# Four MLPs with their matmuls in three single passes over rounded parts and rests

## The chip, the cores and the metric

One NeuronCore of a Trainium2 chip runs the whole kernel. The metric is the device time of one execution in microseconds (us), taken as the median of several runs. TensorE multiplies, VectorE, ScalarE and GpSimd work elementwise, and SyncE issues the DMAs. In the profile they are PE (PEld for its weight loads), DVE, ACT, POOL and SP.

## The reference

Four layers on a residual x of 4 x 256 tokens of width 256 (8 tiles of 128 tokens). Each is an attention followed by an MLP:

- L0: attention over 320 keys, then an MLP behind an RMS norm.
- L1 and L3: two cross attentions each over 64 context keys (four in all, called a = 0 to 3), then an MLP behind a layer norm.
- L2: one cross attention with heads of 16, then an MLP behind a layer norm.

What the change touches is the MLP:

```python
h = _layer_norm(x, ln_mlp_scale, ln_mlp_offset)
h = jax.nn.gelu(h @ w_fc1 + b_fc1, approximate=False) @ w_fc2 + b_fc2
return x + h
```

w_fc1 is 256 x 1024 and w_fc2 1024 x 256, all in float32. L0 and L2 take the tanh form of gelu.

## The kernel before

It is written by hand, engine by engine, and every dependence is a semaphore. Each engine works through one fixed list in order, so an instruction that waits holds up all that stand behind it on its engine. The stages run one after the other: attention 0, mlp(0), keys(0) and tokens(0), keys(1) and tokens(1), mlp(1), attend2, mlp(2), keys(2) and tokens(2), keys(3) and tokens(3), mlp(3). The keys stages fold the weights of 16 heads, streamed by DMA; the tokens stages run over 8 token tiles.

**An MLP** works on four pairs b of token tiles (256 tokens each):

- VectorE: `mlp_spread` (L1367) takes the statistics of both tiles of a pair (L1355 in layer 0, L1357 to L1359 otherwise), `mlp_z` (L1373) writes the normalised z (L1364, L1365) once GpSimd's `power` (L449) has given 1/sqrt. It also adds the down product to x (L1428).
- TensorE: `turn(b)` (L925) transposes z, four 128x128 blocks. `up(b)` (L937) multiplies: for each of 8 blocks f of the hidden width and each half d of the input width, w1's 128x128 block is the stationary operand and hT (128x256) the moving one. In the middle of `up(b)` stands `turn(b + 1)`. `down(b)` (L950) multiplies for each of the two tiles u the 8 blocks of gelu's output hid (stationary) by w2's 128x256 (moving). The order is up(0), up(1), down(0), up(2), down(1), up(3), down(2), in even layers the first two heads' keys of the next stage (L697, L699), down(3).
- ScalarE: `turned(b)` (L1123) writes hT from the transposes, with scale and offset; gelu (L1134) writes hid, one 128x256 block at a time.
- GpSimd: `power`, and `add_row` (L409), which adds the second bias to x, two tiles a pair.

One float32 product of 128x128 by 128x256 stands in the trace as two MATMUL instructions, each with its own weight load. An fp32r product (a float32 rounded to fewer bits) stands as one. The kernel already has such products: the folded keys (L727) are made of a rounded part and the rest, in three passes `PASSES = ((0, 0), (0, 1), (1, 0))`, and attention 0 spreads its queries and keys with fp32r copies (L577, split on VectorE by L1286 and L1288 in `split0`).

**Attention 0** runs 64 steps. In each, GpSimd multiplies the probabilities by the inverse sums (L440), and TensorE turns and uses them (L602, L615). **A tokens stage** has for each tile: scores (L774), softmax on VectorE (L1490 to L1504), half of the multiplication by the inverse sums on GpSimd (L468), transposes (L786), output (L798), and the next tile's h from ScalarE (L1104). **attend2** has z (L1365), queries, softmax and outputs for each tile, and little on GpSimd.

w1 and w2 of a layer are loaded by SyncE (`load_mlp`, L345) as soon as the MLP before has ended, long before they are used. SBUF holds a large tile `arena`, which the stages share.

## Time and profile before

| | us |
|---|---|
| three timed runs | 1070.59, 1075.76, 1069.27 |
| their median | 1070.59 |
| the profiled execution, its own time | 1061.86 |
| its span, first to last instruction | 1060.1 |
| mean granted TensorE clock | 0.986 |

The profile is of one execution. Its time is 0.8% below the median of the timed runs, and 1.76 us of it lie outside the span. Times in the rows below are in us from the span's start; a mean duration of one instruction is in ns. Matmuls overlap, so that the mean duration of one is longer than the step from one to the next.

### The profile page before, as it was taken

Reading aid. Unit: us, or ns where it says so; the run is one execution under the profiler, and the core shown is the slowest. Engines: PE = TensorE matmul, PEld = TensorE weight load, DVE = VectorE, ACT = ScalarE, POOL = GpSimd, SP = SyncE. Lnnn points to the kernel's source line nnn. Section 1 sums busy time; section 2 is a strip of 40 time slices with the busy share of each in tenths; the row PEclk is TensorE's granted clock in tenths of the full one; section 3 lists DMA queues with packets and bytes.
Section 4 is the critical chain, followed back from the end, with each engine's and each line's share of the span. In section 5 each row is a group of like instructions: output and inputs, shape, how many; then the busy total and the mean of one; then the engine's idle time right before and its main releaser. Section 6 shows DMA issues by size and latency. Waiting matters only on the chain.

```text
span 1060.1 us, 15203 instructions
## 1 busy us (share of the span) xinstructions
PE 964.6 (91%) x5272; PEld 775.6 (73%) x5272; DVE 676.3 (64%) x1540; ACT 449.2 (42%) x1108; POOL 341.9 (32%) x381
## 2 busy tenths in 40 slices
PE   5789989799998999989899898899998989989898
PEld 4677778688785677857688687788875678756787
DVE  3788988511989849898511554313989859888510
ACT  3566667432554335633331343422653335533331
POOL 2644535410443324533321020111443324433210
PEclk8899999999999999999999998999999999999999
DMA  9000000000452004310000200200460004200000
GB/s 349 22 1 2 2 1 2 1 1 1 122 181 106 1 1 139 120 60 1 1 1 1 80 1 1 70 1 21 139 219 30 1 20 148 92 1 1 1 11 30
DMA packets 14382, 52.43 MB, mean 49 GB/s; under 512 B 1507, under 2 KB 3043, under 8 KB 13028
## 3 DMA queue, kind: packets, MB, share of 16 engines
q1 hardware_dynamic: 14308, 51.46, 14.3%
q8 instruction: 44, 0.72, 0.3%
q14 instruction: 30, 0.25, 0.1%
HBM read 50.41 MB, written 1.05 MB: 49 GB/s over the span
## 4 chain that ended last, share of the span: by engine, by line
PE 73%; DVE 11%; DMA 8%; issue 4%; ACT 3%; POOL 1%; SPq 0%; DVEq 0%; ACTq 0%
PE ps L950 10%; PE ps L774 9%; PE ps L798 9%; PE ps L937 9%; DMA ring<-in_heads_dram 8%; PE ps L697 4%; PE ps L615 4%; PE ps L699 3%; PE ps L738 3%; PE ps L602 3%; PE ps L727 3%; PE ps L786 2%; PE ps L591 2%; DVE pT_all L1313 2%; PE ps L844 2%
## 5 line engine op out<-in xcount | busy, mean ns | idle before, releaser
L774 PE MATMUL ps<-arena,hT 128*128 128x512 f32 x256 | 117.6, 603 | 15.3 <-ACT hT L1104 15.3
L1428 DVE TENSOR_TENSOR x<-ps,x 128x512 f32<-128x512 f32 x16 | 11.1, 692 | 182.7 <-PE ps L950 182.7
L798 PE MATMUL ps<-arena,pT_all 128*128 128x256 f32 x512 | 116.5, 381 | 7.5 <-ACT pT_all L1181 4.7
L937 PE MATMUL ps<-hT,w 128*128 128x256 f32 x512 | 114.8, 380 | 4.8 <-ACT hT L1123 4.8
L449 POOL TENSOR_TENSOR rstd<-var,neg_half 128x1 f32<-128x1 f32 (+1 forms) x56 | 36.4, 651 | 243.2 <-DVE var L1359 243.2
L950 PE MATMUL ps<-w,arena 128*128 128x256 f32 x512 | 113.3, 379 | 1.8 <-DVE x L1428 1.8
L440 POOL TENSOR_TENSOR arena<-arena,rinv 128x640 f32<-128x640 f32 x64 | 80.2, 1253 | 100.5 <-DVE rinv L1322 100.5
L798 PEld LDWEIGHTS ps<-arena,pT_all 128*128 128x128 f32 x512 | 94.7, 190 | 21.6 <-ACT pT_all L1181 5.7
L937 PEld LDWEIGHTS ps<-hT,w 128*128 128x128 f32 x512 | 96.0, 190 | 18.0 <-issue 5.6
L950 PEld LDWEIGHTS ps<-w,arena 128*128 128x128 f32 x512 | 97.1, 190 | 15.6 <-issue 2.5
L1134 ACT ACTIVATE arena<-ps,cols 128x256 f32<-128x256 f32 x128 | 53.7, 471 | 107.4 <-PE ps L937 107.4
L774 PEld LDWEIGHTS ps<-arena,hT 128*128 128x128 f32 x256 | 48.5, 192 | 65.4 <-issue 46.9
L468 POOL TENSOR_TENSOR prob<-prob,rinv 128x512 f32<-128x512 f32 x32 | 49.5, 1547 | 141.2 <-DVE rinv L1502 141.2
L1188 ACT ACTIVATE prob<-prob 128x512 f32<-128x512 f32 x32 | 20.2, 631 | 143.9 <-DVE prob L1492 143.9
L433 POOL TENSOR_TENSOR vacc<-vacc,vpart 128x256 f32<-128x256 f32 x60 | 44.1, 734 | 108.1 <-ACT vpart L1156 105.8
L1051 ACT ACTIVATE arena<-ps,nb 128x320 f32<-128x320 f32 x128 | 66.4, 523 | 27.0 <-DVE nb L1307 24.7
L697 PE MATMUL ps<-ctxT,ring 128*128 128x256 f32 x256 | 69.3, 393 | 7.5 <-DMA ring<-in_heads_dram 6.9
L1150 ACT ACTIVATE HL<-ps,kvd 128x256 fp32r<-128x256 f32 x64 | 30.5, 476 | 96.3 <-PE ps L699 96.3
L1307 DVE TENSOR_REDUCE nb<-ps 128x2 f32<-128x640 f32 x64 | 52.4, 820 | 25.4 <-PE ps L591 25.3
L602 PE MATMUL ps<-ident,arena 128*128 128x128 f32 x320 | 47.9, 281 | 21.1 <-DVE pT_all L1313 21.0
L727 PE MATMUL ps<-HL,wq 128*128 128x256 f32 x384 | 66.6, 309 | 0.4
L738 PE MATMUL ps<-ring,VT 128*128 128x256 f32 x256 | 65.9, 379 | 0.3 <-DVE x L1428 0.2
(151 smaller groups left out, 1955.0 us busy)
## 6 DMA issues: line engine op xcount, KB each, us to landing
ring<-in_heads_dram SPq DMA_DIRECT2D x64, 512.0 KB, 3.5
w<-in_w_dram SPq DMA_DIRECT2D x8, 1024.0 KB, 7.3
x<-in_x_dram SPq DMA_DIRECT2D x1, 1024.0 KB, 10.0
lnb<-in_lnb_dram SPq DMA_DIRECT2D x4, 256.0 KB, 9.2
ring<-in_wp_dram SPq DMA_DIRECT2D x1, 1024.0 KB, 4.9
out_dram<-x SPq DMA_DIRECT2D x4, 256.0 KB, 2.3
arena<-in_kinT_dram SPq DMA_DIRECT2D x1, 960.0 KB, 7.3
brow<-in_brow_dram SPq DMA_DIRECT2D x1, 768.0 KB, 11.0
```

Of the source, the lines that this page charges most:

```text
L440: g.tensor_tensor(w, w, rinv[:, n % 2, 0:2].unsqueeze(2).broadcast_to([P, 2, KEYS0]), ALU.mult)\
L602: last = nc.tensor.transpose(ps[:, 4 + c // 4, (c % 4) * P:(c % 4 + 1) * P], prob0[:, n % 4, c * P:(c + 1) * P], ident[:, :])
L697: mm(ps[:, k, 0:B * C], w[:, d * P:(d + 1) * P], ctxT[:, 0, d, :], start=(d == 0), stop=(d == 1))
L727: last = mm(ps[:, A_BANKS[k][d], 0:B * C], wq[:, k, c, d * P:(d + 1) * P], KT[:, k, e, :], start=(p == 0), stop=(p == 2))
L738: last = mm(ps[:, 5 + k, g * D:(g + 1) * D], VT[:, k, g * P:(g + 1) * P], ring[:, n % RING, 768:1024], start=True, stop=True)
L774: last = mm(ps[:, half, :], hT[:, k, d, 0:P], A[:, d, b // 2, cols_of, sl, :].rearrange("p r s k -> p r (s k)"), start=(d == 0), stop=(d = ...
L798: last = mm(ps[:, 6, 0:D], pT[:, k, c, :], VW[:, b, c, :], start=(c == 0), stop=(c == PAIRS - 1))
L937: last = mm(ps[:, f // 2, (f % 2) * 256:(f % 2 + 1) * 256], w1[:, d, f * P:(f + 1) * P], hT[:, k, d, :], start=(d == 0), stop=(d == 1))
L950: last = mm(ps[:, 5 + u, 0:D], hid[:, k, f, u * P:(u + 1) * P], w2[:, f, :], start=(f == 0), stop=(f == FT - 1))
L1051: last = a_(prob0[:, n % 4, e * KEYS0:(e + 1) * KEYS0], ps[:, 2 * (n % 2) + e, 0:KEYS0], ACT.Exp, bias=nb[:, n % 2, e:e + 1], scale=-1.0, ...
L1134: a_(hid[:, b % 2, f, :], ps[:, f // 2, (f % 2) * 256:(f % 2 + 1) * 256], gelu, bias=col(bias, f)).then_inc(hid_ready, 1)
L1307: v.tensor_reduce(nb[:, n % 2, :], ps[:, j:j + 2, 0:KEYS0], AX.X, ALU.min).then_inc(nb_ready, 1)
```

## The change

Every float32 product of the four MLPs is replaced by three fp32r products: high x high, high x low, low x high. The high part is the value rounded to fp32r, the low part the float32 difference, written as fp32r.

- **Weights.** GpSimd splits w1 and w2 into w1H, w1L, w2H, w2L with `split_weights(l, j)`, 16 instructions a layer on 128x512 each (even j a copy, odd j a subtraction). Layer 0's stand in attention 0 behind the multiplications of even steps 24 to 54; those of layers 1 and 3 in tokens(1) and tokens(3), two behind each tile's multiplication; those of layer 2 in attend2, four behind each of the tiles 4 to 7.
- **Activations.** VectorE splits hT (128x512) in `mlp_split(l, b)`, a copy and a subtraction; TensorE's `up(b)` waits for `hs_ready` where it waited for `hm_ready`. `mlp_split(l, 0)` stands ahead of the statistics of pair 1, and `mlp_split(l, b + 1)` behind the high copies of pair b's first half.
- **gelu's output.** VectorE writes hidH in four copies of 128x512 a pair (`hidden_high`), GpSimd the rest hidL in four subtractions of 128x512, in place of hid. `down(b)` waits for hidL, pair of blocks by pair of blocks.
- **Order.** VectorE's addition of pair b's result moves behind the high copies of pair b + 1. GpSimd's `power` of pair b + 2 moves to the head of pair b, and its memset (3.66 us, layer 1) from pair 0 to pair 1.
- **Places.** Several tiles share addresses (`overlay`), and x0 and prob0 move within `arena`.

The diff, without the semaphores' declarations:

```diff
+        def overlay(name, shape, dt):
+            with nc.sbuf_tensor(name, shape, dt) as tile:
+                return tile
+        arena_r = overlay("arena_r", [P, 16384], F32R)
-        x0 = arena[:, 11776:13824].rearrange("p (t n) -> p t n", t=TILES)
-        prob0 = arena[:, 13824:13824 + 4 * 2 * KEYS0].rearrange("p (k n) -> p k n", k=4)
+        prob0 = arena[:, 11776:11776 + 4 * 2 * KEYS0].rearrange("p (k n) -> p k n", k=4)
+        x0 = arena[:, 14336:16384].rearrange("p (t n) -> p t n", t=TILES)
-        copies = sb("copies", [P, 4, 2, 2, P], F32R)
-        K0 = sb("K0", [P, 3, KEYS0], F32R)
-        Q0 = sb("Q0", [P, 3, 2, S], F32R)
+        first_r = overlay("first_r", [P, 2048 + 3 * KEYS0 + 6 * S], F32R)
+        copies = first_r[:, 0:2048].rearrange("p (j w c n) -> p j w c n", j=4, w=2, c=2)
+        K0 = first_r[:, 2048:2048 + 3 * KEYS0].rearrange("p (k n) -> p k n", k=3)
+        Q0 = first_r[:, 2048 + 3 * KEYS0:2048 + 3 * KEYS0 + 6 * S].rearrange("p (k e n) -> p k e n", k=3, e=2)
+        PN = H * C + H
+        prob = sb("prob", [P, 2, PN])
+        wq = sb("wq", [P, 2, 2, D], F32R)
+        VT = sb("VT", [P, 2, B * C])
+        u = sb("u", [P, 2, D])
+        vpart = sb("vpart", [P, 2, D])
...
+        w1L = overlay("w1L", [P, DH, F], F32R)
+        w2L = overlay("w2L", [P, FT, D], F32R)
+        w1H = sb("w1H", [P, DH, F], F32R)
+        w2H = sb("w2H", [P, FT, D], F32R)
-        VT = sb("VT", [P, 2, B * C])
-        wq = sb("wq", [P, 2, 2, D], F32R)
+        hL = overlay("hL", [P, 2, DH, 2 * P], F32R)
+        hH = sb("hH", [P, 2, DH, 2 * P], F32R)
-        PN = H * C + H
-        prob = sb("prob", [P, 2, PN])
+        hidL = arena_r[:, 0:4096].rearrange("p (k f n) -> p k f n", k=2, f=FT)
+        hidH = arena_r[:, 9728:13824].rearrange("p (k f n) -> p k f n", k=2, f=FT)
...
-                sp.dma_start(w1[:, :, :], t["w1"][l]).then_inc(in_mlp, 16)
-                sp.dma_start(w2[:, :, :], t["w2"][l]).then_inc(in_mlp, 16)
+                sp.dma_start(w1[:, :, :], t["w1"][l]).then_inc(in_w1, 16)
+                sp.dma_start(w2[:, :, :], t["w2"][l]).then_inc(in_w2, 16)
...
                         pool.wait_ge(vacc_ready, n)
                         g.tensor_tensor(vacc[:, :], vacc[:, :], vpart[:, k, :], ALU.add).then_inc(vacc_ready, 1)
 
+            def split_weights(l, j):
+
+                c, high = j // 2, j % 2 == 0
+                part = slice(c % 2 * 512, c % 2 * 512 + 512)
+                two = slice(2 * (c - 4), 2 * (c - 4) + 2)
+                w = w1[:, c // 2, part] if c < 4 else w2[:, two, :]
+                wH = w1H[:, c // 2, part] if c < 4 else w2H[:, two, :]
+                wL = w1L[:, c // 2, part] if c < 4 else w2L[:, two, :]
+                if j == 0:
+                    pool.wait_ge(in_w1, 16 * (l + 1))
+                if j == 8:
+                    pool.wait_ge(in_w2, 16 * (l + 1))
+                if high:
+                    g.tensor_copy(wH, w).then_inc(w_step, 1)
+                else:
+                    pool.wait_ge(w_step, 8 * l + c + 1)
+                    g.tensor_tensor(wL, w, wH.bitcast(F32), ALU.subtract).then_inc(w_split, 1)
+
             pool.wait_ge(in_w0, 16 * 4)
             for n in range(TILES * PAIRS):
 
...
                     .then_inc(w0_pool, 1)
                 if n < TILES:
                     add_row(x0, n, "L0_out_b")
+                if 24 <= n < 56 and n % 2 == 0:
+                    split_weights(0, (n - 24) // 2)
 
             def power(phase, i, width):
 
...
                     pm = prob[:, k, 0:HALF].rearrange("p (h c) -> p h c", c=C)
                     g.tensor_tensor(pm, pm, rinv[:, k, 0:H // 2].unsqueeze(2).broadcast_to([P, H // 2, C]), ALU.mult)\
                         .then_inc(p_ready, 1)
+                    if a % 2 == 1:
+                        split_weights(a, 2 * n)
+                        split_weights(a, 2 * n + 1)
 
             def mlp_rows(l, name):
                 power(f"M{l}", 0, 2)
                 power(f"M{l}", 1, 2)
                 for b in range(B):
-                    if 1 <= b < B - 1:
-                        power(f"M{l}", b + 1, 2)
+                    if b + 2 < B:
+                        power(f"M{l}", b + 2, 2)
                     for n in (2 * b, 2 * b + 1):
                         if l > 0:
                             pool.wait_ge(zm_ready, l * B + b + 1)
                         add_row(x, n, name)
-                    if l == 1 and b == 0:
+                    for pair in range(FT // 2):
+                        two = slice(2 * pair, 2 * pair + 2)
+                        pool.wait_ge(hidH_ready, (l * B + b) * FT // 2 + pair + 1)
+                        g.tensor_tensor(hidL[:, b % 2, two, :], hid[:, b % 2, two, :], hidH[:, b % 2, two, :].bitcast(F32),
+                                        ALU.subtract).then_inc(hidL_ready, 1)
+                    if l == 1 and b == 1:
 
                         pool.wait_ge(rows_done, rows_before("M1"))
                         g.memset(arena[:, 5632:9728], 0.0).then_inc(kc_clear, 1)
...
                     power("L2", n + 2, 1)
                 pool.wait_ge(z_ready, 2 * TILES + n + 1)
                 add_row(x, n, "L2_cproj_b")
+                if n >= 4:
+                    for j in range(4 * n - 16, 4 * n - 12):
+                        split_weights(2, j)
             mlp_rows(2, "L2_proj_b")
             keys(2, range(2))
             first_norms(2)
...
 
                 def up(b):
                     k = b % 2
-                    pe.wait_ge(hm_ready, base + b + 1)
+                    pe.wait_ge(hs_ready, base + b + 1)
+                    if b == 0:
+                        pe.wait_ge(w_split, 8 * l + 4)
                     for f in range(FT):
                         if b >= 1 and f % 2 == 0:
 
                             pe.wait_ge(hid_ready, (base + b - 1) * FT + f + 2)
+                        block = slice(f * P, (f + 1) * P)
+                        o = ps[:, f // 2, (f % 2) * 256:(f % 2 + 1) * 256]
                         for d in range(DH):
-                            last = mm(ps[:, f // 2, (f % 2) * 256:(f % 2 + 1) * 256], w1[:, d, f * P:(f + 1) * P],
-                                      hT[:, k, d, :], start=(d == 0), stop=(d == 1))
+                            mm(o, w1H[:, d, block], hH[:, k, d, :], start=(d == 0), stop=False)
+                            mm(o, w1H[:, d, block], hL[:, k, d, :], start=False, stop=False)
+                            last = mm(o, w1L[:, d, block], hH[:, k, d, :], start=False, stop=(d == 1))
                         last.then_inc(f1_ps, 1)
                         if f == FT // 2 - 1 and b + 1 < B:
                             turn(b + 1)
 
                 def down(b):
                     k = b % 2
-                    pe.wait_ge(hid_ready, (base + b + 1) * FT)
-                    if b >= 1:
+                    if b == 0:
+                        pe.wait_ge(w_split, 8 * l + 8)
+                    else:
                         pe.wait_ge(rows_done, rows_before(f"M{l}") + b)
                     for u in range(2):
+                        at = slice(u * P, (u + 1) * P)
                         for f in range(FT):
-                            last = mm(ps[:, 5 + u, 0:D], hid[:, k, f, u * P:(u + 1) * P], w2[:, f, :],
-                                      start=(f == 0), stop=(f == FT - 1))
+                            if u == 0 and f % 2 == 0:
+                                pe.wait_ge(hidL_ready, ((base + b) * FT + f) // 2 + 1)
+                            o = ps[:, 5 + u, 0:D]
+                            mm(o, hidH[:, k, f, at], w2H[:, f, :], start=(f == 0), stop=False)
+                            mm(o, hidH[:, k, f, at], w2L[:, f, :], start=False, stop=False)
+                            last = mm(o, hidL[:, k, f, at], w2H[:, f, :], start=False, stop=(f == FT - 1))
                     last.then_inc(f2_ps, 1)
 
                 turn(0)
...
+            def mlp_split(l, b):
+                n = l * B + b
+                dve.wait_ge(hm_ready, n + 1)
+                v.tensor_copy(hH[:, b % 2, :, :], hT[:, b % 2, :, :]).then_inc(hH_step, 1)
+                dve.wait_ge(hH_step, n + 1)
+                v.tensor_tensor(hL[:, b % 2, :, :], hT[:, b % 2, :, :], hH[:, b % 2, :, :].bitcast(F32), ALU.subtract)\
+                    .then_inc(hs_ready, 1)
+            def hidden_high(l, b, pair):
+                dve.wait_ge(hid_ready, (l * B + b) * FT + 2 * pair + 2)
+                two = slice(2 * pair, 2 * pair + 2)
+                v.tensor_copy(hidH[:, b % 2, two, :], hid[:, b % 2, two, :]).then_inc(hidH_ready, 1)
+                def add(b):
+                    dve.wait_ge(f2_ps, base + b + 1)
+                    dve.wait_ge(xb_ready, TILES * XB_AT[f"M{l}"] + 2 * b + 2)
+                    v.tensor_tensor(x[:, 2 * b:2 * b + 2, :], ps[:, 5:7, 0:D], x[:, 2 * b:2 * b + 2, :], ALU.add)\
+                        .then_inc(rows_done, 1)
+                mlp_split(l, 0)
...
                     if b + 2 < B:
                         mlp_spread(l, b + 2)
                         mlp_z(l, b + 2)
-                    if l == 1 and b == B - 1:
-                        dve.wait_ge(zmT_ps, base + B)
-                        dve.wait_ge(rows_done, rows_before("M1") + B // 2 + 1)
-                        first_z2()
-                    if l % 2 == 0 and b == B - 1:
-                        weights(l, 0)
-                        keys_rest(l, 0)
-                    dve.wait_ge(f2_ps, base + b + 1)
-
-                    dve.wait_ge(xb_ready, TILES * XB_AT[f"M{l}"] + 2 * b + 2)
-                    v.tensor_tensor(x[:, 2 * b:2 * b + 2, :], ps[:, 5:7, 0:D], x[:, 2 * b:2 * b + 2, :], ALU.add)\
-                        .then_inc(rows_done, 1)
+                    hidden_high(l, b, 0)
+                    hidden_high(l, b, 1)
+                    if b + 1 < B:
+                        mlp_split(l, b + 1)
+                    hidden_high(l, b, 2)
+                    hidden_high(l, b, 3)
+                    if b >= 1:
+                        add(b - 1)
+                if l == 1:
+                    dve.wait_ge(zmT_ps, base + B)
+                    dve.wait_ge(rows_done, rows_before("M1") + B // 2 + 1)
+                    first_z2()
+                if l % 2 == 0:
+                    weights(l, 0)
+                    keys_rest(l, 0)
+                add(B - 1)
 
             def first_z2():
 
```

## Rows read from the trace of the kernel before

**Rows 1.** The page: busy time of the engines, and the chain that ended last.

```profile
PE 964.6 (91%) x5272; PEld 775.6 (73%) x5272; DVE 676.3 (64%) x1540; ACT 449.2 (42%) x1108; POOL 341.9 (32%) x381
...
PE 73%; DVE 11%; DMA 8%; issue 4%; ACT 3%; POOL 1%; SPq 0%; DVEq 0%; ACTq 0%
```

**Rows 2.** Windows, first MLP: us; busy us of PE, PEld, DVE, ACT, POOL; clock, DMA share, GB/s.

```profile
204.10:265.40 61.30, 60.55 (x286) 53.09 (x287) 10.38 (x28) 19.93 (x45) 10.59 (x16) 1.00 0.00 1
```

**Rows 3.** The chain in order of time, first MLP: start us, us, what.

```profile
219.05 6.92 PE ps L950 x32
```

**Rows 4.** Groups of instructions by form: busy us, mean ns | idle before, releaser.

```profile
L937 PE MATMUL ps<-hT,w 128*128 128x256 f32 x512 | 114.8, 380 | 4.8 <-ACT hT L1123 4.8
...
L925 PE MATMUL ps<-ident,z 128*128 128x128 f32 x64 | 9.8, 276 | 4.5 <-DVE z L1365 3.5 <-DVE z L1364 1.0
...
L1504 DVE TENSOR_TENSOR prob<-prob,rinv 128x512 f32<-128x512 f32 x32 | 22.1, 692 | 1.1
...
L1260 DVE TENSOR_SCALAR copies<-arena,cols 128x512 fp32r<-128x512 f32 x4 | 1.7, 482 | 8.5 <-DMA bo<-in_bo_dram 8.5
...
L440 POOL TENSOR_TENSOR arena<-arena,rinv 128x640 f32<-128x640 f32 x64 | 80.2, 1253 | 100.5 <-DVE rinv L1322 100.5
...
L409 POOL TENSOR_TENSOR x<-x,brow 128x256 f32<-128x256 f32 x40 | 28.9, 740 | 6.6 <-DVE z L1365 6.6
...
L430 POOL COPY vacc<-vpart 128x256 f32<-128x256 f32 x4 | 1.6, 396 | 67.6 <-ACT vpart L1156 67.6
```

**Rows 5.** Timeline of the weight loads, narrow windows around L727's second burst.

```profile
285.08 0.88 PEld L727 LDWEIGHTS ps<-HL,wq 128*128 128x128 f32 x6
...
285.30 0.31 PEld L727 LDWEIGHTS ps<-HL,wq 128*128 128x128 f32 x2
...
285.89 0.19 PEld L738 LDWEIGHTS ps<-ring,VT 128*128 128x128 f32 x1
```

**Rows 6.** Timeline of the last MLP's start: start us, us, engine, what [idle before <-releaser].

```profile
990.44 0.73 DVE L1365 TENSOR_SCALAR z<-x,mv,rstd 128x256 f32<-128x256 f32 x2
...
996.33 0.43 DVE L1357 BATCH_NORM_STATS2 stat<-x 128x6 f32<-128x256 f32 x1
...
997.47 3.69 PE L937 MATMUL ps<-hT,w 128*128 128x256 f32 x16 [1.20 <-ACT hT L1123]
...
997.98 0.70 POOL L449 TENSOR_TENSOR rstd<-var,neg_half 128x2 f32<-128x2 f32 x1 [9.49 <-DVE var L1359]
998.63 1.46 POOL L409 TENSOR_TENSOR x<-x,brow 128x256 f32<-128x256 f32 x2
998.71 1.54 DVE L1365 TENSOR_SCALAR z<-x,mv,rstd 128x256 f32<-128x256 f32 x2 [0.81 <-POOL rstd L449]
...
1008.34 0.60 PE L925 MATMUL ps<-ident,z 128*128 128x128 f32 x4
```

**Rows 7.** Timeline of VectorE and GpSimd in attention 0.

```profile
109.60 1.39 DVE L1288 TENSOR_TENSOR HL<-arena,HL 128x256 fp32r<-128x256 f32 x1
...
128.83 1.25 POOL L440 TENSOR_TENSOR arena<-arena,rinv 128x640 f32<-128x640 f32 x1 [1.32 <-DVE rinv L1322]
```

**Rows 8.** Timeline of TensorE: the first scores of two token stages.

```profile
805.97 3.70 PE L774 MATMUL ps<-arena,hT 128*128 128x512 f32 x8 [2.28 <-ACT hT L1104]
...
936.03 5.40 PE L774 MATMUL ps<-arena,hT 128*128 128x512 f32 x8 [2.27 <-ACT hT L1104]
```

**Rows 9.** The windows view: attention 2's middle, and behind the slow start of Rows 8.

```profile
630.00:640.00 10.00, 9.37 (x73) 8.80 (x72) 5.91 (x10) 4.44 (x9) 0.73 (x1) 1.00 0.00 0
...
938.00:940.00 2.00, 2.00 (x3) 0.67 (x2) 1.85 (x6) 0.00 (x0) 1.73 (x3) 0.50 0.04 8
```

**Rows 10.** Timeline of a middle token tile of attention L1/1.

```profile
352.20 0.41 DVE L1365 TENSOR_SCALAR z<-x,mv,rstd 128x256 f32<-128x256 f32 x1
...
357.00 0.48 ACT L1104 ACTIVATE hT<-ps,ones 128x256 f32<-128x256 f32 x1
...
358.88 1.02 PE L774 MATMUL ps<-arena,hT 128*128 128x512 f32 x2
```

12 lines of the change are left out of this document (8 added, 4 removed).

## The prediction, made before the changed kernel had run

> **What bounds the kernel now.** I read the page first: its busy shares and its chain that ended last [rows 1]. TensorE is busy for 964.6 us of 1060.1 and carries 73% of the chain. VectorE has 64% and GpSimd 32%, so there is room on both, on average. Then the windows by stage. In the first MLP [rows 2] TensorE is busy for 60.55 of 61.30 us at a granted clock of 1.00 (its upper level, 2.4 GHz), while VectorE works for 10.38 and GpSimd for 10.59. An MLP is therefore bound by the matmuls alone. The chain [rows 3] shows its unit: the up or the down product of a token pair is 32 MATMULs (16 products of 128x128 by 128x256, each two instructions in f32) and takes 6.92 us. That is 0.432 us a product. The grouped lines [rows 4] count 512 instructions for L937 alone; L950 has as many, so there are 512 products in the four MLPs, 221 us of the span.
>
> **What a single rounded pass costs.** L727 already multiplies fp32r operands of the same shape, 128x128 by 128x256. Its mean duration hides the pitch, so I looked at single weight loads [rows 5]: of a burst of six that starts at 285.08, the second starts at 285.30 and the f32 load of the next line, behind the sixth, at 285.89. Five steps in 0.59 us are 0.118 us a pass; three passes are 0.354 us, against 0.432. **TensorE gains 512 x 0.078 = 40.0 us.** The first step of that burst is 0.22, because it still follows an f32 product; taken over the whole burst the pitch would be 0.135 (0.81/6), and two thirds of the gain would be gone (512 x 0.027 = 14 us left). In the MLPs 24 or 48 passes follow each other, so I take the inner steps. The Trainium skill ("TensorE: Matmul & The Clock Gate", Back-to-back issue gap) has N/2.4 + 2.5 ns for a warm pass, an estimate of 0.109 us here; by it the gain would be 53.7 us. The trace shows 0.118, and the sum goes by the trace.
>
> **Start of each MLP.** Today ScalarE writes hT and the first up product starts at once: 997.47, behind hT's last activation [rows 6]. Now VectorE stands between: a rounding copy of 128x512 (0.48, by L1260, the fp32r write of this size) and a subtraction (0.69, by L1504, two inputs of this size) [rows 4], with two handoffs of some 0.07. That is 1.3 us, fully exposed, for ScalarE's table load lies beside it as before. **Four times: -5.2 us.**
>
> **The second pair's wait.** Up(1) follows up(0) on TensorE with nothing between, and needs the split of pair 1. VectorE's order is now: split(0), statistics(1), z(1), statistics(2), z(2), high copies 0 and 1 of pair 0, split(1). Counted from up(0)'s first product: statistics take 1.5 us (996.33 to the start of GpSimd's power at 997.98, less the handoff), the power 0.70, two z's 0.73 alone [rows 6]. So z(1) is ready at 3.0, just at the turn in up(0)'s middle (24 x 0.118 = 2.8). Statistics(2) end at 4.5, power(2) at 5.3. Then z(2) meets GpSimd's row additions: the same two z's took 1.54 us instead of 0.73 where L409 ran beside them [rows 6], so 6.9. Two copies of 0.48 end at 7.9. From here GpSimd's remainders hidL run beside VectorE's rounding and subtraction, both of which read and write SBUF, and each of the two waits for one.
> What a remainder of 128x512 takes on GpSimd no row shows. From below it is 1.02 (L440's 1.253 for 640 elements with a broadcast second input, times 512/640), from above 1.48 (twice L409's 0.74 for 256, two full inputs) [rows 4]. I take 1.27, nearer to twice L409, because both inputs are full and the fixed part is paid once. Then pair 1's split is ready at about 10.7. Up(0) ends at 0.2 + 48 x 0.118 + 0.44 = 6.3, where 0.44 is the turn in its middle, L925's four transposes (0.60 at 1008.34) less the tail that overlaps [rows 6]. TensorE waits 4.4 to 4.7 us, where it waits nothing today: **-4.5 us, four times -18.0.** Without any blocking (z(2) at 6.1, copies, rounding and subtraction straight behind, 8.5) the wait would be 2.2; with 1.48 per remainder, 5.
> That the two engines block each other is this trace's own: L1288, 128x256 with two SBUF inputs, takes 1.39 us beside a multiplication on GpSimd [rows 7], against 0.69 for twice the size [rows 4]. The Trainium skill ("SBUF — State Buffer", Who interferes with whom) makes it an exclusive lock for the whole instruction. Rows 6 show less: two z's and two additions took 1.54 us where one after the other is 0.73 + 1.46 = 2.19. By the skill's full lock each MLP would lose another 0.8 (four meetings ahead of up(1), 0.2 later each), an estimate of 3.2 in all.
>
> **What goes.** Today the turn of pair 3 waits for z(3), because VectorE adds pair 0's result first; this is TensorE's idle time ahead of L925, 4.5 us less 0.3 at the start of the first MLP [rows 4]. In the new order z(3) comes before that addition. **+4.2 us.** In the last pair nothing changes: down(3) waits for add(2) in odd layers as before.
>
> **The remaining blocks.** A period (up and down of a pair) is 2 x 48 x 0.118 = 11.3 us. GpSimd has 4 x 1.27 + two rows 1.46 + a power 0.70 = 7.2, VectorE 5 x 0.48 + 0.69 + 1.5 + 0.73 + 0.69 = 6.0. What can block each other is GpSimd's 7.2 and VectorE's copies, subtraction and z's, 3.8, together 11.0. They fit, barely, and the remainders have slack, since down(b) comes a whole up (5.7 us) after pair b's gelu. I count no wait there. The 3.66 us memset in layer 1 goes into the same slack.
>
> **The clock.** A wait of 4.5 us is long. At 936.03 TensorE had idled 2.27 us, and the eight MATMULs behind took 5.40 us, where 3.70 is usual [rows 8]; the granted clock from 938 to 940 was 0.50, the lower level (1.2 GHz) [rows 9]. That is 1.7 us for one gap; the same gap ahead of 805.97 went without. With gaps twice as long I take it in three of four MLPs: **-5.1 us**; between 0 and 8 for the range.
>
> **Weights split ahead, on GpSimd.** Sixteen instructions a layer: eight copies of 128x512 (0.4 for 256 by L430, so 0.6) and eight remainders (1.27). Layer 0's lie in attention 0, one behind every even step from 24 to 54. Gaps behind the even steps of L440 are 1.32 us at least, as ahead of 128.83 [rows 7], so 1.27 just fits and the next multiplication is not late; a few of VectorE's fp32r splits (L1288) will be blocked longer. -1.0 (0 to -6). Layers 1 and 3 have two behind each token tile's multiplication: at 352.20 VectorE's z will be blocked by up to 1.3 us and drags the softmax along. ScalarE's h for the next tile ends at 357.48 and is used at 358.88 [rows 10], so 1.4 us of slack hides almost all of it: -1.0 (0 to -5). Layer 2's lie in the middle of attention 2, where GpSimd works 0.73 us in ten [rows 9]: 0. No DMA is added; w1 and w2 land where they did, long before.
>
> **Sum.** 40.0 + 4.2 - 5.2 - 18.0 - 5.1 - 2.0 = 13.9 us less. The profiled execution took 1061.86 us, span 1060.1, so it would be 1048.0. The three timed runs have a median of 1070.59, 0.8% more; the difference applies to it as well: **1056.7 us**, a ratio of 0.987.
>
> **Rivals.**
> A. The splits hide: GpSimd and VectorE interleave finely, remainders take 1.0, up(1) waits 2.2 us and the clock holds. 40.0 + 4.2 - 5.2 - 8.8 - 2 = 28 us, 1042 us. For it: means of 32% and 64%, and the incomplete blocking of rows 6. Against: the order of VectorE's list, which is fixed. Chance 0.22.
> B. The pipeline never catches up: 11.0 of 11.3 us leaves nothing, so up(2) and up(3) also wait, 1.5 us each, once more with the lower clock: 4 x (3.0 + 0.5) = 14 us, all the gain, 1070. For it: strict order on both engines. Against: the slack of one up. Chance 0.20.
> C. Slower: GpSimd writes fp32r far more slowly than f32. One mechanism, at hidL and the weight splits. No row has GpSimd writing fp32r. VectorE's fp32r writes cost the same as f32 ones, which speaks against. From 2.0 us a remainder it decides: then the four in a period (8.0) plus rows and power (2.2) and VectorE's 3.8 pass 13.8 us, today's period. At 2.5 the MLPs lose 11 us over today, attention 0 some 8 x 1.2 = 10 for remainders past the gap, the token tiles 5: 26 us more, 1096. Chance 0.10.
> That three passes are no faster than f32 (a pitch of 0.144 or more) would have the same sign; I hold it below 0.03, within C's share.
>
> **How the numbers follow.** The forecast (1048 to 1065) has 0.48, A 0.22, B 0.20, C 0.10. What a measurement of this kernel can tell from no change is about 1%, 10.7 us. Faster by more: A and four fifths of the forecast, 0.60. Within 1%: the rest of the forecast and most of B, 0.25. Slower: C and the tail of B, 0.15. The range leaves out C and the best end of A: 1038 to 1074.
>
> **What would show it.** L937 and L950's successors: 768 MATMULs each, all steps 0.118, a product block 5.7 us. The first up of each MLP some 1.3 us later behind hT. A gap of 4 to 5 us ahead of up(1) in each MLP, ended by VectorE's subtraction, with a granted clock near 0.5 behind it. No gap ahead of the turn of pair 3. GpSimd's remainders near 1.27 us, L440's starts in attention 0 unmoved. The forecast is wrong if the pitch is above 0.13, if a remainder takes over 1.6 us, or if down() waits for hidL.

## The result, and the profile after

The changed kernel takes 1053.1 us (median of 4 runs, 1051.3 to 1059.7), the kernel before 1069.9 in the same session: a ratio of 0.985, 95% interval 0.981 to 0.990. The forecast was 1056.7 us and 0.987, so the forecast case came true. Its terms were nearly right one by one, with errors that cancel in the sum, and nearly half of what three passes gain was lost to one wait that another order takes away.

The profiled execution of the changed kernel took 1059.66 us with a span of 1057.9. That is only 2.2 us less than the 1060.1 of the kernel before, where the medians differ by 16.8. The page and two windows over the same stage, attention 2, say why. First the page of the changed kernel (busy time, chain by engine):

```profile
PE 950.5 (90%) x5784; PEld 779.5 (74%) x5784; DVE 759.7 (72%) x1636; ACT 448.6 (42%) x1108; POOL 473.1 (45%) x509
...
PE 63%; DVE 27%; issue 4%; ACT 3%; DMA 1%; POOL 1%; SPq 0%; DVEq 0%; ACTq 0%
```

Windows of attention 2 in the kernel before:

```profile
584.20:674.60 90.40, 78.57 (x492) 67.69 (x493) 45.04 (x90) 34.41 (x72) 7.57 (x11) 0.94 0.06 24
```

The same stage in the changed kernel:

```profile
580.90:678.00 97.10, 84.16 (x492) 72.01 (x492) 45.32 (x89) 35.49 (x72) 22.18 (x27) 0.88 0.07 25
```

And in a second execution of the same changed kernel, profiled for run e1:

```profile
575.60:666.30 90.70, 77.52 (x493) 66.93 (x493) 45.42 (x90) 35.59 (x72) 22.19 (x27) 0.94 0.07 27
```

GpSimd does 14.6 us more here in both executions of the changed kernel (its weight splits), yet one takes 97.1 us and the other 90.7, as the kernel before. What differs is the granted clock, 0.88 against 0.94. The trace of before was a lucky one: its span is shorter than that of all 26 later executions of that kernel (1061.8 to 1077.2 us), and its clock, 0.986, is near the top of theirs (0.971 to 0.987). A comparison of two single traces was therefore worth little outside the MLPs. Inside them it holds, and I cut both traces at the first up product and at the last result row of each MLP:

```
us                 before  changed  changed (e1)
MLP 0               61.95    56.09    56.23
MLP 1               60.03    54.54    55.46
MLP 2               62.37    57.73    55.71
MLP 3               60.03    54.55    55.92
all four           244.4    222.9    223.3
rest of the span   815.7    835.0    818.6
```

21.1 to 21.5 us are gained in the MLPs; some 1.15 us before each of them is lost to the later start (4.6 in all). The weight splits cost something too, which shows where the clock stays at 1.00 in both kernels. These are my cuts: attention 0 from GpSimd's multiplication (L440, now L479) of step 23 to that of step 56, and tokens(1) from its first scores to its last output:

```
us at clock 1.00             before   changed kernel and its variants
attention 0, steps 23 to 56   89.09    90.22 to 90.25 (all ten traces with all splits)
                                       89.73 (e6 and e7, half the splits)
tokens(1)                     71.38    72.34 to 72.40 (e1, e3, e5, e10)
```

Tokens(3) took 72.4 at that clock (e3, e9), so it loses about as much as tokens(1). The splits cost 1.15 + 2 x 1.0 = 3.2 us. The lines show where: in each pair the kernel before comes first, then e1.

```profile
107.22 0.49 DVE L1288 TENSOR_TENSOR HL<-arena,HL 128x320 fp32r<-128x320 f32 x1
...
105.92 0.78 DVE L1349 TENSOR_TENSOR HL<-arena,HL 128x320 fp32r<-128x320 f32 x1
```

```profile
460.47 0.49 DVE L1491 TENSOR_SCALAR mx<-mx 128x8 f32<-128x8 f32 x1
...
454.36 1.21 DVE L1580 TENSOR_SCALAR mx<-mx 128x8 f32<-128x8 f32 x1
```

In attention 0 four steps (24, 28, 40 and 44) are 0.29 us longer; in step 28, shown here, one of VectorE's fp32r splits stands beside GpSimd's copy of w1. In tokens(1) the step from tile 1's scores to tile 2's grew from 7.07 to 7.79 us: `mx`, an instruction of 8 elements, waits there until the subtraction w1L on GpSimd is through.

21.3 - 4.6 - 3.2 = 13.5. The medians show 16.8 (their interval, 11 to 20 us, holds both), and in a second session (e1) 21.5. Where the rest comes from is not shown: the four stages that fold streamed weights each vary by 2 to 4 us from trace to trace.

The groups of the MLP's lines, changed kernel (they answer to L937, L925 and L409 in [rows 4]):

```profile
L991 PE MATMUL ps<-hH,w1H 128*128 128x256 f32 x256 | 78.6, 307 | 22.2 <-DVE hL L1476 12.8 <-issue 9.4
...
L975 PE MATMUL ps<-ident,z 128*128 128x128 f32 x64 | 10.2, 283 | 0.2 <-DVE z L1425 0.2
...
L1476 DVE TENSOR_TENSOR hL<-hT,hH 128x512 fp32r<-128x512 f32 x16 | 19.7, 1232 | 0.5
...
L528 POOL TENSOR_TENSOR arena_r<-arena,arena_r 128x512 fp32r<-128x512 f32 x64 | 85.7, 1350 | 44.6 <-DVE arena_r L1483 44.6
...
L472 POOL TENSOR_TENSOR w1L<-w,w1H 128x512 fp32r<-128x512 f32 x16 | 20.3, 1270 | 1.0
...
L469 POOL CAST w1H<-w 128x512 fp32r<-128x512 f32 x16 | 10.3, 643 | 0.0
```

Read the idle column first. Ahead of L991 TensorE stood for 22.2 us: 9.4 are the four starts (2.35 each; the profile names no releaser there, but in the last MLP VectorE's subtraction ends at 1000.65, 0.10 before the first product), 12.8 the waits ahead of up(1), ended by VectorE's subtraction. The turn (L975) no longer waits: 0.2 where it was 4.5. A remainder (the rest of a value, a subtraction) takes 1.27 us on GpSimd for the weights (L472) and 1.35 in the MLP.

The start of the last MLP, timeline of the changed kernel (it answers to [rows 6]):

```profile
1000.75 0.55 PE L991 MATMUL ps<-hH,w1H 128*128 128x256 f32 x1 [2.35 <-issue]
...
1004.04 0.28 PE L991 MATMUL ps<-hH,w1H 128*128 128x256 f32 x1
...
1004.40 0.28 PE L991 MATMUL ps<-hH,w1H 128*128 128x256 f32 x1
...
1005.89 1.49 POOL L430 TENSOR_TENSOR x<-x,brow 128x256 f32<-128x256 f32 x2
...
1006.03 1.50 DVE L1426 TENSOR_SCALAR z<-x,mv,rstd 128x256 f32<-128x256 f32 x2 [0.88 <-POOL rstd L490]
...
1007.45 0.75 DVE L1483 CAST arena_r<-arena 128x512 fp32r<-128x512 f32 x2
...
1007.95 2.79 POOL L528 TENSOR_TENSOR arena_r<-arena,arena_r 128x512 fp32r<-128x512 f32 x2 [0.57 <-DVE arena_r L1483]
...
1008.12 1.49 DVE L1474 CAST hH<-hT 128x512 fp32r<-128x512 f32 x1
1009.65 1.64 DVE L1476 TENSOR_TENSOR hL<-hT,hH 128x512 fp32r<-128x512 f32 x1
...
1011.34 0.58 PE L991 MATMUL ps<-hH,w1H 128*128 128x256 f32 x1 [2.76 <-DVE hL L1476]
...
1019.95 0.28 PE L1010 MATMUL ps<-w2H,arena_r 128*128 128x256 f32 x1
...
1020.30 0.28 PE L1010 MATMUL ps<-w2H,arena_r 128*128 128x256 f32 x1
```

Three passes of up take 0.36 us (1004.04 to 1004.40), 0.120 each, three of down 0.35 (1019.95 to 1020.30), 0.117 each. Up(1) begins 10.59 us after up(0). VectorE is busy without a gap from 1006.03, first with z(2), which pair 1 doesn't need, and then with a cast and a subtraction that last 3.17 us (1008.12 to 1011.29) beside GpSimd's remainders.

The granted clock fell at both ends, by the windows of the changed kernel:

```profile
1002.00:1004.00 2.00, 2.00 (x11) 2.00 (x11) 1.19 (x4) 0.31 (x1) 0.70 (x1) 0.51 0.04 8
...
1012.00:1014.00 2.00, 2.00 (x11) 2.00 (x11) 1.30 (x6) 0.00 (x0) 2.00 (x2) 0.50 0.00 0
```

The first of the two is free: it makes up(0) slower (7.3 us instead of 6.0), but up(1) can't start before 10.6 anyway. In e1, where up(0) ran at full clock, the wait is 4.07 instead of 2.76 and up(1) starts at 10.58.

### The profile page after: what moved, and what is told of

It reads as the page before. It is cut to its first block, busy times and chain, and to the rows that moved or that the text cites. A ratio compares the mean times of both kernels' runs of the same rounds, so it can differ in the third digit from the quotient of the medians.

```text
span 1057.9 us, 16451 instructions
## 1 busy us (share of the span) xinstructions
PE 950.5 (90%) x5784; PEld 779.5 (74%) x5784; DVE 759.7 (72%) x1636; ACT 448.6 (42%) x1108; POOL 473.1 (45%) x509
## 4 chain that ended last, share of the span: by engine, by line
PE 63%; DVE 27%; issue 4%; ACT 3%; DMA 1%; POOL 1%; SPq 0%; DVEq 0%; ACTq 0%
PE ps L826 10%; PE ps L850 9%; PE ps L667 4%; DVE wq L1460 3%; DVE wq L1459 3%; PE ps L654 3%; PE ps L1010 3%; PE ps L1012 3%; PE ps L1011 3%; PE ps L991 2%; DVE arena L1547 2%; PE ps L992 2%; PE ps L993 2%; PE ps L838 2%; PE ps L643 2%
## 5 line engine op out<-in xcount | busy, mean ns | idle before, releaser
L826 PE MATMUL ps<-arena,hT 128*128 128x512 f32 x256 | 122.7, 625 | 16.7 <-ACT hT L1165 16.7
L479 POOL TENSOR_TENSOR arena<-arena,rinv 128x640 f32<-128x640 f32 x64 | 80.3, 1255 | 86.6 <-DVE rinv L1383 86.4
L850 PEld LDWEIGHTS ps<-arena,pT_all 128*128 128x128 f32 x512 | 94.7, 190 | 21.5 <-ACT pT_all L1242 5.6
L528 POOL TENSOR_TENSOR arena_r<-arena,arena_r 128x512 fp32r<-128x512 f32 x64 | 85.7, 1350 | 44.6 <-DVE arena_r L1483 44.6
L991 PE MATMUL ps<-hH,w1H 128*128 128x256 f32 x256 | 78.6, 307 | 22.2 <-DVE hL L1476 12.8
L992 PE MATMUL ps<-hL,w1H 128*128 128x256 f32 x256 | 76.3, 298 | 0.0
L993 PE MATMUL ps<-hH,w1L 128*128 128x256 f32 x256 | 76.0, 297 | 0.0
L1010 PE MATMUL ps<-w2H,arena_r 128*128 128x256 f32 x256 | 72.2, 282 | 1.6 <-DVE x L1492 1.6
L1011 PE MATMUL ps<-w2L,arena_r 128*128 128x256 f32 x256 | 71.6, 280 | 0.0
L1012 PE MATMUL ps<-w2H,arena_r 128*128 128x256 f32 x256 | 71.6, 280 | 0.0
L991 PEld LDWEIGHTS ps<-hH,w1H 128*128 128x128 f32 x256 | 53.4, 208 | 24.0 <-DVE hL L1476 13.6
L654 PE MATMUL ps<-ident,arena 128*128 128x128 f32 x320 | 47.7, 281 | 22.2 <-DVE pT_all L1374 22.1
```

Of the source, the lines that this page charges most:

```text
L479: g.tensor_tensor(w, w, rinv[:, n % 2, 0:2].unsqueeze(2).broadcast_to([P, 2, KEYS0]), ALU.mult)\
L528: g.tensor_tensor(hidL[:, b % 2, two, :], hid[:, b % 2, two, :], hidH[:, b % 2, two, :].bitcast(F32), ALU.subtract).then_inc(hidL_ready, 1)
L654: last = nc.tensor.transpose(ps[:, 4 + c // 4, (c % 4) * P:(c % 4 + 1) * P], prob0[:, n % 4, c * P:(c + 1) * P], ident[:, :])
L826: last = mm(ps[:, half, :], hT[:, k, d, 0:P], A[:, d, b // 2, cols_of, sl, :].rearrange("p r s k -> p r (s k)"), start=(d == 0), stop=(d = ...
L850: last = mm(ps[:, 6, 0:D], pT[:, k, c, :], VW[:, b, c, :], start=(c == 0), stop=(c == PAIRS - 1))
L991: mm(o, w1H[:, d, block], hH[:, k, d, :], start=(d == 0), stop=False)
```

## The experiments

Eleven runs were made; e1 is the changed kernel again and e10 is e2 again. Theory T: the wait ahead of up(1) comes from the order of VectorE's list and from GpSimd's slowing of two VectorE instructions; the clock falls behind it. Rival R: GpSimd has too much to do (rests, rows, weight splits), so that the loss only moves when the order is changed.

**e1, the changed kernel again**, for the clock.

> The changed kernel once more, beside the kernel before: about 1053 us, ratio 0.985. What it has to tell is the clock: the profiled execution of the kernel before had 7 stretches at half clock and that of the changed kernel 17, with +6.7 us in attention 2 alone. If that is the change's doing, this run's trace has attention 2 at about 97 us again, against 90.5 in the kernel before; if it is one execution's luck, it lies near 90 to 92.

Measured: 1048.2 us, ratio 0.981 (0.973 to 0.988). Attention 2 took 90.7: luck, not the change. Over the 13 traces kept, that stage varies between 89.6 and 97.7 us, with 10 to 25 us of it at the lower clock. It shows no relation to what GpSimd has to do there: the same work gave 90.7 and 97.7.

**e2, other order.**

```diff
 VectorE, for b in range(B):
-    if b + 2 < B: mlp_spread(l, b + 2); mlp_z(l, b + 2)
     hidden_high(l, b, 0)
-    hidden_high(l, b, 1)
     if b + 1 < B: mlp_split(l, b + 1)
+    hidden_high(l, b, 1)
+    if b + 2 < B: mlp_spread(l, b + 2); mlp_z(l, b + 2)
     hidden_high(l, b, 2); hidden_high(l, b, 3)
     if b >= 1: add(b - 1)
 GpSimd, for b in range(B):
-    power(b + 2); add_row(2 * b); add_row(2 * b + 1)
-    four rests hidL
+    two rests hidL; power(b + 2); two rests hidL
+    add_row(2 * b); add_row(2 * b + 1)
```

> Same work, other order: in each pair of chunks VectorE writes the first copies of gelu's output and then at once the next pair's parts and rests, ahead of the z of the pair after it and of the last three copies; GpSimd takes two rests first and the rows of the residual last. Theory T (the 2.8 to 4.5 us ahead of up(1) are VectorE's queue and its blocking by GpSimd, not the amount of work): the rest of pair 1 comes some 3 us earlier, the idle time ahead of up(1) goes to 1 us or less in each of four MLPs, and the half clock behind it with it: 4 x (2.5 to 3.8) + up to 4 x 1.7 = 10 to 20 us less than the changed kernel, 1033 to 1043 us. Rival R (GpSimd's throughput is the bound of the MLP: rests, rows and powers follow each other without a gap): the wait only moves to down(0), down(1) or up(2), and the time stays within 3 us of 1053.

Measured: 1032.5 us, ratio 0.965 (0.959 to 0.971). Lines and the last MLP's window of this kernel:

```profile
L991 PE MATMUL ps<-hH,w1H 128*128 128x256 f32 x256 | 74.4, 291 | 9.4 <-issue 9.4
...
L975 PE MATMUL ps<-ident,z 128*128 128x128 f32 x64 | 10.5, 289 | 1.4 <-DVE z L1425 0.8 <-DVE z L1426 0.5
```

```profile
971.00:1023.00 52.00, 47.97 (x399) 47.08 (x397) 25.98 (x53) 18.59 (x41) 30.05 (x27) 1.00 0.05 16
```

Nothing is left ahead of L991 but the four starts; the wait went, and of it only 1.4 us came back, at the turn. The clock is 1.00 over the last MLP. MLP 1 and 3 take 49.35, all four 204.1: 19 us less than in the changed kernel, 40.3 less than before. GpSimd does the same work as in the changed kernel, in another order. R falls.

**e3, blocking taken away.** GpSimd's list waits once, ahead of the rests of pair 0.

```diff
+                    if b == 0:
+                        pool.wait_ge(hs_ready, l * B + 2)
                     for pair in range(FT // 2):
```

> The changed kernel, with GpSimd's rests of pair 0's gelu held back until the parts and rests of pair 1 are written. Theory T's second half (the cast and the subtraction of pair 1, 1.49 and 1.64 us beside GpSimd's subtraction against 1.07 and 1.23 in the mean, are slowed by it): both fall to their undisturbed 0.8 to 1.2 us, the idle time ahead of up(1) from 2.76 to about 1.5 to 2.2 us; down(0) then waits for its rests (4 x 1.3 us from then on, against 5.6 us of up(1)), so about 0 to 1 us more there, and the whole lies between 1046 and 1053 us. Rival R (GpSimd's amount of work is the bound): holding it back by some 3 us costs that much, 4 x 3 = 12 us more, 1065 us.

Measured: 1038.6 us, ratio 0.971 (0.965 to 0.976), better than either theory had it (by 7 us). Timeline of this kernel at the end of up(0), last MLP:

```profile
990.61 0.41 DVE L1476 CAST hH<-hT 128x512 fp32r<-128x512 f32 x1
991.06 0.69 DVE L1478 TENSOR_TENSOR hL<-hT,hH 128x512 fp32r<-128x512 f32 x1
991.67 1.84 DVE L1485 CAST arena_r<-arena 128x512 fp32r<-128x512 f32 x2
```

```profile
991.80 0.39 PE L993 MATMUL ps<-hH,w1H 128*128 128x256 f32 x1 [2.06 <-DVE hL L1478]
```

The cast takes 0.41 instead of 1.49 and the subtraction 0.69 instead of 1.64; the wait goes from 4.07 (e1, up(0) at full clock as here) to 2.06. So GpSimd's slowing was half of the wait, 2.0 us, and the position in the list the other half. A wait added to the engine with the most new work made the kernel 9.6 us faster than e1, which ran beside it (14.6 against the first session): down(0) had the whole of up(1) as slack and never waited. The MLPs take 212.2 us in sum, 11 less than in e1; 7.6 of it is the earlier start of up(1) (by 1.7 to 2.0 us in each), the rest clock.

**e4, more work in GpSimd's weight splits**: the high copies of layers 1 to 3 are written three times.

```diff
-                    g.tensor_copy(wH, w).then_inc(w_step, 1)
+                    for again in range(3 if l > 0 else 1):
+                        if again > 0: pool.wait_ge(w_step, ...)
+                        g.tensor_copy(wH, w).then_inc(w_step, 1)
```

> The high copies of the weights of layers 1 to 3 written three times instead of once: 2 x 0.64 = 1.28 us more of GpSimd for each of eight chunks, 3 x 8 x 1.28 = 30.8 us of GpSimd in all, beside attention and tokens. If the splits ahead are hidden, as my sum has it in attention 2, nothing comes of it there; in the tokens stages, where the stage table shows about 0.5 us each for 4 chunks of splits (1.92 us each), another 0.67 of it, 0.3 us per stage: 0 to 2 us in all, 1053 to 1055 us. The rival (GpSimd's splits stand on the path in the stages of tokens and attention, and are the 2 to 7 us by which those stages grew): the added work costs as its share, 10 to 15 us, 1063 to 1068 us.

Measured: 1047.3 us, ratio 0.981 (0.974 to 0.987), the same as e1 beside it, with 30 us more on GpSimd:

```profile
L474 POOL CAST w1H<-w 128x512 fp32r<-128x512 f32 x40 | 25.1, 627 | 1.5
```

So more copies in layers 1 to 3 are hidden: tokens(1) and tokens(3) take 73.67 and 73.09 us, against 73.77 and 73.02 in traces with as long a stretch at the lower clock (the changed kernel and e1). This doesn't show that the splits are free. What costs in tokens(1) is a subtraction, and e4 added copies only, and it left attention 0's splits as they were.

**e5, TensorE kept busy** with 16 unused products ahead of up(0) and ahead of up(1). The wait for w1's splits moves ahead of the MLP's first turn.

```diff
+                    for i in range((16, 16, 0, 0)[b]):
+                        mm(ps[:, 7, 0:D], w1H[:, 0, 0:P], w1H[:, 1, 0:D], start=True, stop=True)
                     pe.wait_ge(hs_ready, base + b + 1)
```

> The changed kernel with 16 unused products of 128x256 (about 1.9 us at full clock) on TensorE ahead of the wait for the rests of pair 0, and 16 ahead of that for pair 1, in each of four MLPs. What is waited for is the same. If the half clock at the start of up(0) and of up(1) is due to TensorE's idle time before them (my clock term, 1.7 us for each stretch), the stretches at half clock go: up to 2 x 1.7 x 4 = 13.6 us less, 1036 to 1042 us, and the later MLPs measure 51 to 53 us where the changed kernel has 54.5 to 55.9. Rival: the clock falls for other reasons (the load of three passes with all engines at work), or the unused products delay up() by as much: within 3 us of the changed kernel, 1047 to 1053 us.

Measured: 1050.1 us, ratio 0.983 (0.981 to 0.985). As a total that is a miss: no different from the changed kernel (0.985 and 0.981 in its two sessions). Timeline and window at up(1) of the last MLP:

```profile
997.72 2.08 PE L982 MATMUL ps<-w1H 128*128 128x256 f32 x16
...
1001.97 0.39 PE L993 MATMUL ps<-hH,w1H 128*128 128x256 f32 x1 [2.17 <-DVE hL L1479]
```

```profile
1002.00:1004.00 2.00, 2.00 (x17) 2.00 (x18) 1.86 (x8) 0.30 (x1) 1.67 (x2) 1.00 0.00 0
```

Here up(1) runs at 1.00. Its length, between first and last of its L991 instructions, was 5.9 us in three of the four MLPs and 7.4 in one, where the changed kernel had 7.2 to 8.0 in all four. What is waited for is the same, so in three of four cases the idle time made the clock fall behind that wait; in the fourth, MLP 2, it fell in spite of the products. MLP 1 and 3 come to 53.35 (54.5 and 54.6, in e1 55.5 and 55.9). The sum over the MLPs is 218.8, 4 us less than 222.9, which is below what the medians can separate here. The fall at up(0) went too, but that one costs nothing in this order, so only about half of the 13.6 us that I expected was there to win.

**e6 and e7, each product alone.** In e6 down alone goes in three passes (no hH, hL and w1 splits; up reads hT and w1); in e7 up alone (no hidH, hidL and w2 splits; down reads gelu's f32 output and w2).

> Only the second product in three passes; up in fp32 as before, no parts and rests of the activations, and w1 not split. If the halves add up: 256 x 0.078 = 20.0 us gained, no start, no wait ahead of up(1), pair 3's turn as before: 1070 - 20 = 1050 us, each later MLP 60.0 - 5.0 = 55.0 us. The rival (GpSimd's rests of gelu's output hold down() back, or their blocking of VectorE costs z and the rows of the residual more than is gained): 1056 us or more, and an idle time ahead of down() in its lines.

> Only the first product in three passes; down in fp32 as before, no rounded copy and rest of gelu's output, w2 not split. 20.0 us gained in up, less the start (4 x 1.3), less a wait ahead of up(1) which stays although GpSimd has nothing to do but powers and rows: VectorE writes z of the pair after it first, so 1.5 us and the half clock behind it 1.7 us, 4 x 3.2 = 12.8: 1070 - 20 + 5.2 + 12.8 = 1068 us, 2 to 6 us less where pair 3's turn is gained too: 1062 to 1068. If instead GpSimd's rests alone make the wait ahead of up(1), there is none here: 1055 us or less.

Measured: e6 1044.9 us, ratio 0.978 (0.975 to 0.982); e7 1058.3, ratio 0.990 (0.989 to 0.992). The half with down alone is better than I expected, and no slower than the whole change (1053.1 and 1048.2): up in three passes, added to it in this order, brought nothing. Lines of e6, then of e7:

```profile
L993 PE MATMUL ps<-hT,w 128*128 128x256 f32 x512 | 116.5, 384 | 4.6 <-issue 4.6
...
L1010 PE MATMUL ps<-w2H,arena_r 128*128 128x256 f32 x256 | 74.6, 291 | 1.6 <-DVE x L1492 1.6
```

```profile
L1470 DVE TENSOR_TENSOR hL<-hT,hH 128x512 fp32r<-128x512 f32 x16 | 12.7, 796 | 0.6
...
L1468 DVE CAST hH<-hT 128x512 fp32r<-128x512 f32 x16 | 7.6, 475 | 25.4 <-ACT hT L1178 25.4
```

In e6 no gap but the old start and the last addition is left, although VectorE and GpSimd write all of gelu's parts. In e7 the cast and the subtraction take 0.48 and 0.80 us in the mean, against 1.07 and 1.23 in the changed kernel: it is the rests of gelu that slow them. Its up(1) still starts 7.9 us after up(0) in MLP 1, where the clock stayed at 1.00 and e2 needs 6.35: 1.5 us is what the list's order costs without any rests. By my cut of the traces:

```
all four MLPs, us   before 244.4
e6 down alone              221.0   -23.4
e7 up alone                227.4   -17.0
both, order of the change  223.3   -21.1  (e1)
both, order of e2          204.1   -40.3
the same again             206.9   -37.5  (e10)
```

The parts add up to 40.4, close to e2's 40.3, but partly by luck: the sum counts the turn of pair 3 twice (4.2 us too much), has e7's wait in it (1.5 us an MLP), and each trace has one to three stretches at the lower clock. In the change's order both together bring 16 to 19 us less than in e2's. That is the price of one order.

**e8, e2's order with 16 unused products ahead of up(0).**

> The order of the second run together with 16 unused products ahead of up(0) alone, the one idle time that this order leaves in the MLP's start. If the half clock at up(0) comes from the 2.3 us of idle time before it: 4 x 1.7 = 6.8 us less than the 1032.5 us of that order, 1025.7; with the unused products partly in the way of up(0), 1026 to 1030. If it has another cause: 1031 to 1035.

Measured: 1032.8 us, ratio 0.967 (0.965 to 0.969): nothing gained; MLP 1 and 3 take 49.40 and 49.38, as without them. In e2 the clock had not fallen behind the 2.35 us of those two starts, so there was nothing to save. In MLP 0, where it had, e8 has 52.15 us and e2 53.61; that 1.5 is too little for the medians. In e10, again e2's order, it had fallen at up(0) in three of four, and its MLPs take 206.9 against 202.7 in e8. With products ahead of up(0) (e5 and e8) the clock fell at none of eight starts. That is worth 1.4 to 4.2 us in the traces, and the medians, 1032.8 against 1032.5 and 1030.0, don't show it.

**e9, only VectorE's half of e2's order.**

> Only VectorE's half of the second run's order; GpSimd's list stays that of the changed kernel (power of the pair after it, rows of the residual, then four rests). Theory: the wait ahead of up(1) was half VectorE's queue (z of pair 2 ahead of the parts of pair 1) and half the slowing by GpSimd; with the queue gone first, the parts of pair 1 are written before GpSimd's rests of pair 0 begin, and the idle time ahead of up(1) is 0 to 1 us. GpSimd's rests then begin later, behind a power that waits for pair 2's spread: 0 to 2 us of wait move to down(0). Each later MLP 50 to 52 us, the whole 1034 to 1040. Rival (the saving of that run came from GpSimd's new order, which frees the rests early): the later MLPs stay at 54 us or more, 1048 us or more.

Measured: 1036.0 us, ratio 0.968 (0.963 to 0.973). Up(1) starts 6.35 us after up(0) in MLP 1, as in e2; nothing moved to down(0), which never waits. What moved is small, turn(2) in the middle of up(1):

```profile
518.90 0.35 PE L991 MATMUL ps<-hH,w1H 128*128 128x256 f32 x1 [2.35 <-issue]
...
529.20 0.66 PE L975 MATMUL ps<-ident,z 128*128 128x128 f32 x4 [0.92 <-DVE z L1426]
```

MLP 1 takes 50.35 us, 1.0 more than in e2. VectorE's order is nearly all of the gain.

**e10 and e11, a better version.** e10 is e2 again. e11 adds, in up(0)'s first block alone, the four passes that need only hH first, behind a wait for hH, and the two over hL last.

> The order of the second run once more, in more rounds, beside the next: 1028 to 1036 us, ratio 0.962 to 0.970, later MLPs 49.4 us. Nothing is left to wait for in them: what they take is 384 passes at 0.118 us and the turns.

> That order, and in the first block of up(0) the four passes that need only the rounded part come first; TensorE starts when that part is written and not when the rest is, 0.69 us later. The idle time ahead of up(0) goes from 2.35 us to 1.7, and the two passes over the rest follow 4 x 0.12 = 0.48 us later: 0.48 us less in each of four MLPs, 1.9 us in all, 1026 to 1034 us. The rival (the start is covered, or the wait inside the block costs what the earlier start brings): the idle time is split in two parts whose sum is 2.35 us, and the time is the same as that of the run beside it.

Measured: e10 1030.0 us, ratio 0.962 (0.957 to 0.966), with MLPs of 49.39, 53.23 and 50.77 where I expected 49.4 for each: in the last two up(0) ran in part at the lower clock. e11 took 1027.5, ratio 0.959 (0.955 to 0.963). One of e11's six executions took 3460 us; there is no trace of it, and its cause is open. Timeline of e11:

```profile
978.14 0.36 PE L994 MATMUL ps<-hH,w1H 128*128 128x256 f32 x1 [1.62 <-issue]
...
981.85 0.66 PE L975 MATMUL ps<-ident,z 128*128 128x128 f32 x4 [0.39 <-DVE z L1437]
```

The idle time at the start fell from 2.35 to 1.62, but the turn in the middle of up(0) now waits for z(1), 0.39. From the start of the idle time to the last result the last MLP takes 51.5 us, 51.7 in e2. So 0.2 and not 0.48 is gained per MLP, which the medians can't tell. The order of e2 is the version that beats both kernels: 1030 to 1032 us.

## Why the prediction was right, step by step

- **What bounds the kernel: right.** The MLPs were matmul-bound, and all the gain that can be located lies in them.
- **Three passes, +40.0: right.** A product took 0.35 us in down and 0.36 in up instead of 0.432: 256 x 0.082 + 256 x 0.072 = 39.4. e2 as a whole shows 40.3 us in the MLPs (e10 37.5) of the 43.6 that this and the turn's 4.2 make; most of the rest is the lower clock at up(0), 1.4 us in one MLP of e2 and three of e10, and 1.4 at the turns. The estimate of 0.109 (the Trainium skill, "TensorE: Matmul & The Clock Gate", Back-to-back issue gap, which has that formula for a matmul by itself) was too low for these passes, at 0.117 and 0.120, and the row of before was the better guide.
- **Start of each MLP, -5.2: nearly.** The idle time went from 1.20 to 2.35, 4 x 1.15 = 4.6. Cast and subtraction took 0.43 and 0.69.
- **Wait ahead of up(1), -18.0: right in place, time and cause; a little too large.** Predicted were 10.7 us from up(0) to up(1); measured 10.60, 10.56 and 10.59 in MLPs 1 to 3 and 9.61 in MLP 0. With the 6.35 that TensorE needs (e2) that is 3 x 4.23 + 3.3 = 16.0. What I had split as 2.2 without and 4.5 with GpSimd's blocking is 2.06 (e3) and 4.07 (e1). (In e3 z(2) still met the row additions, so 2.06 is the wait without the rests and not without all blocking.) The 1.27 us of a remainder came out as 1.27 for the weights and 1.35 to 1.40 in place. That 10.7 was hit to 0.1 is partly luck: VectorE's copies were through at 7.45 and not at 7.9, and the cast and the subtraction then took 3.2 us and not 2.8.
- **Turn of pair 3, +4.2: right.** L925's 4.5 us are L975's 0.2, and e6 and e7 got it too.
- **No wait at the remaining blocks: right.** Up(2) and up(3) never wait, which was rival B's condition, and down() never waits for hidL. What rival A's chance rested on, that the engines hardly disturb each other, didn't hold.
- **Clock, -5.1: right in size, the count a guess.** It rested on one gap that was followed by the lower clock and one that wasn't, and on three of four MLPs; it was four. Up(1) took 7.2 to 8.0 us between its first and last L991, at full clock 5.9 (e5): 1.2 to 2.1 us in each of four MLPs, 5.9 in all. I had missed that the clock also falls at up(0), behind the start; it costs nothing only because up(1) waits anyway.
- **Weight splits, -2.0: right in kind, too small.** Measured are 1.15 in attention 0 (forecast 1.0), through a few of VectorE's fp32r splits as I had it, and 1.0 in each of two tokens stages (forecast 1.0 for both). "L440's starts unmoved" was wrong by that 1.15. The tiles in the middle of tokens(1) are unmoved at 7.98 us, as the slack of 1.4 us had it; tile 1's step to tile 2 and the last tile are not. e4 alone would have made the term look like nothing.

By measured terms: 39.4 + 4.2 - 16.0 - 5.9 = 21.7 in the MLPs, against 21.1 to 21.5 in the traces; less 4.6 for the starts and 3.2 for the splits it is 13.9, the sum of the forecast. That the two agree to 0.1 is luck: 2.0 too much for the wait and 0.6 for the starts cancel 0.6 too little for the pitch (the passes' step), 0.8 for the clock and 1.2 for the splits. The medians show 3 us more than these terms, and 8 more in e1's session; no run here says from where.

Where I was wrong in the experiments: e3, e6 and e7 came out 4 to 7 us better than expected. For e3 I left out that a shorter wait also saves part of the half clock behind it (3.5 us in the MLPs), and I counted from a wait of 2.76 that a slow up(0) had shortened; up(1) started 2.0 us sooner. For e6 I left out the turn of pair 3 (4.2). For e7 I charged 1.7 us of half clock in each MLP, and its up(1) ran at 1.00 in all four. In e5 and e8 I took the clock's fall at up(0) for certain, and in e5 for a cost.

## What to carry to other kernels

A step that feeds the engine at the bound belongs ahead of work that is due a whole block later, in the list of its engine: moving z(2) behind the next pair's split was worth nearly as much as the three-pass change itself (e2 15.7 us less than e1, e1 21.5 less than the kernel before). When one engine's large elementwise instructions have slack, let them wait on purpose until the other engine's urgent ones are through. Try the halves of a change alone; here half of it was no slower than all of it, a sign of loss that needs no trace. And when added work costs nothing, ask whether it is of the kind that could: e4's copies were free, the subtractions beside them weren't.
